# Attention logits from high and low float32r parts, outputs turned beside their accumulators, and logits alternating with transposes

## Chip, cores and metric

One core of a Trainium2 chip. The metric is the device time of one launch in microseconds (us); a comparison is made on the median of several runs.

## What is computed

A decoder layer on x of 2048 x 256: x = LN(x + attention(x)); x = LN(x + cross_attention(x, ctx)); x = LN(x + ffn(x)). The change concerns the first attention, of 16 heads of 64, whose logits carry a contextual position term (CoPE). For each head:

```python
sim = einsum('bid,bjd->bij', q, k) * d ** (-0.5)
G = sigmoid(sim); P = minimum(flip(cumsum(flip(G))), T_MAX - 1)
E = einsum('bnc,ct->bnt', q, pos_emb)
w = P - floor(P)
sim = sim + w * E[ceil(P)] + (1 - w) * E[floor(P)]
out = softmax(sim) @ v        # heads side by side, then @ Wout + b_out
```

All inputs are float32. Only the last 176 keys of a row have a position below the cap, so the kernel adds the term in a window of 176 columns (W).

## The kernel before

`attention()` works in 128 groups (G): 16 heads times 8 groups, each group being two units of 128 queries (u = 0, 1) against all 2048 keys. The five engines run hand-written programs side by side, tied by semaphores; nothing but these programs sets the order of the work. In PSUM, `Sc` has four banks of logits, `near` one bank of window logits, `ring` two banks used in turn by everything that ScalarE copies out, and `out` one accumulator bank.

For group g, in the order of TensorE's `body` (L581):

- `logits` (L544) of unit 0: one float32 matmul of 128 queries by 512 keys per bank. The head has 64 channels, so a matmul uses 64 rows of the array; even blocks of keys lie on partitions 0 to 63 and odd ones on 64 to 127 of `qk`, the queries `q_now` on both, and two matmuls on different row halves stand in a row. The wait for `exp_done` guards `Sc`, which the exponentials of the last unit still read.
- `turn` (L575) of unit 0 of group g-1: a matmul with `fold` adds and turns the two halves of its outputs into a `ring` bank. Then four times `transposes` (L552) of unit 1 of g-1, each of which fills a `ring` bank and waits until ScalarE has emptied the one before the last; `outputs` (L566), 16 matmuls into `out`, with `project` (L500) and `project_values` (L513) for a group 8 ahead after the first four.
- `logits` of unit 1, `turn` of unit 1 of g-1, four `transposes` of unit 0, `window` (L522) for group g+2, `outputs` of unit 0.

A group thus has two halves, one from unit 1's logits to unit 0's, one back.

ScalarE (`body` in its block) copies `out` to `halves` (L424), scales a turned output into `attn` (`scale`, L418), copies transposes to `probsT` (L409), copies a projection to `qk` (L368) and values to `V` (L382), takes a tanh of the window (L388), copies the table of position terms (L392), and does the exponentials (`exps`, L430) in two halves of 1024 columns when VectorE's `bias` (L765) is ready. VectorE takes maxima of 1024 columns (`half_max`, L748), adds the position term to the last columns (`add_window`, L755), and between these works through the position chain of the next group: scans (L674, L689), masks (L702), masked shifts (L712, L735) and small operations. GpSimd does one product per group (L348). SP issues the DMAs: `load_far` (L237) for the window's queries two groups ahead, `load_tile` (L258), and `load_now` (L241, L242), two DMAs that fill `q_now` for group g+1 once all logits of g are done:

```python
wait_apart(sp, bank_full, g * 4 + 4, waited)
load_now(g + 1, not odd)
```

Groups 112 to 119 project queries and keys alone, groups 120 to 127 nothing. Eight projection steps run ahead of the first group. TensorE's program for heads 1 to 12 is a loop over two heads, with `head` written out twice; each has an inner loop over two written-out bodies and two more bodies behind it, so that eight bodies are written out in it. After `attention()` come `general_attention()`, whose branches are not taken here, and `cross_and_ffn()`, from about 2180 us to the end; neither is touched.

## Time and profile before

| | us |
|---|---|
| median of 3 runs | 2649.62 (2647.76 to 2652.51) |
| the profiled execution's own time | 2652.94 |
| its span, first to last instruction | 2651.1 |
| TensorE busy (matmuls) | 2472.1, 93% |
| VectorE busy | 2006.4, 76% |
| ScalarE busy | 1615.9, 61% |
| GpSimd busy | 190.4, 7% |
| DMA engines, mean share | 10.1% |
| mean granted TensorE clock | 0.985 of 2.4 GHz |

Busy times are of the whole span; the first attention takes about 2177 us of it. A float32 matmul shows as two records and two weight loads, a transpose as one. Records of matmuls that follow one another overlap, so the time of a piece is read from its start to the start of the next.

### The profile page before, as it was taken

The page shows a single profiled execution, that of the slowest core. Times are in us where ns is not written, and L with a number is a line of the kernel's source. Part 1 is how long each engine was busy: PE and PEld are TensorE (multiplying, and loading weights), DVE is VectorE, ACT ScalarE, POOL GpSimd, SP SyncE. Part 2 cuts the span into 40 slices and gives each one's busy share as a digit, 9 for nine tenths or more (in the row PEclk, how much of TensorE's full clock was granted, in tenths as well). Part 3 has the DMA queues.
Part 4 walks back from the last instruction along what each step waited for, and adds up shares of the span by engine and source line. Part 5 has one row for each costly group of instructions (what it writes and reads, how often), then busy time and mean ns, then how long its engine had stood idle before and what let it go on. Part 6 is the DMA issues. An engine that isn't in the chain of part 4 may idle for free. (4 is left out here: it accounts for less than half of the span.)

```text
span 2651.1 us, 64197 instructions
## 1 busy us (share of the span) xinstructions
PE 2472.1 (93%) x18687; PEld 1691.1 (64%) x18687; DVE 2006.4 (76%) x5179; ACT 1615.9 (61%) x3383; POOL 190.4 (7%) x289
## 2 busy tenths in 40 slices
PE   7999998999899989998999999999999988999997
PEld 5666665666566656666666566666666656777776
DVE  6888888888888888888888888888899960232322
ACT  4666666666666666666666666666666663444442
POOL 0000000000000000000000000000000000111111
PEclk9999999999999999999999999999999998999998
DMA  2010101010101010100101110101001002100100
GB/s 68 20 33 20 34 20 32 20 34 20 32 20 34 20 32 21 32 21 21 29 24 29 25 29 24 29 24 29 22 21 40 21 17 68 34 26 34 36 26 6
DMA packets 96567, 74.74 MB, mean 28 GB/s; under 512 B 24590, under 2 KB 92303, under 8 KB 96464
## 3 DMA queue, kind: packets, MB, share of 16 engines
q1 hardware_dynamic: 96464, 73.15, 10.1%
q8 instruction: 90, 1.47, 0.2%
q14 instruction: 13, 0.11, 0.0%
HBM read 14.26 MB, written 2.10 MB: 6 GB/s over the span
## 5 line engine op out<-in xcount | busy, mean ns | idle before, releaser
L748 DVE TENSOR_REDUCE mx<-Sc 128x1 f32<-128x1024 f32 x512 | 621.5, 1214 | 160.2 <-PE Sc L544 159.7
L552 PE MATMUL ring<-ident,probs 128*128 128x128 f32 x4096 | 620.9, 284 | 115.2 <-ACT attn L418 65.3
L409 ACT ACTIVATE probsT<-ring 128x512 f32<-128x512 f32 x1024 | 584.7, 596 | 132.1 <-PE ring L552 129.2
L552 PEld LDWEIGHTS ring<-ident,probs 128*128 128x128 f32 x4096 | 446.3, 145 | 258.3 <-ACT attn L418 127.0
L430 ACT ACTIVATE probs<-Sc,nbias 128x1024 f32<-128x1024 f32 x512 | 565.6, 1117 | 4.7 <-DVE nbias L765 4.7
L544 PE MATMUL Sc<-qk,q_now 64*128 64x512 f32 x2048 | 539.4, 637 | 22.4 <-issue 16.0
L566 PE MATMUL out<-probsT,V_now 128*64 128x128 f32 x8192 | 530.0, 277 | 0.0
L566 PEld LDWEIGHTS out<-probsT,V_now 128*64 128x64 f32 x8192 | 439.5, 137 | 76.3 <-ACT probsT L409 57.9
L712 DVE COPY_PREDICATED z<-mask,z 128x224 f32<-128x224 int16 (+5 forms) x768 | 389.7, 507 | 34.4
L418 ACT ACTIVATE attn<-ring,rsum 128x64 f32 (+1 forms) x256 | 80.3, 314 | 436.5 <-PE ring L575 420.7
L544 PEld LDWEIGHTS Sc<-qk,q_now 64*128 64x128 f32 x2048 | 173.6, 188 | 217.8 <-issue 217.8
L348 POOL TENSOR_TENSOR prod<-cut,z 128x350 f32<-128x350 f32 x128 | 118.3, 924 | 2036.2 <-DVE z L735 2036.2
L575 PEld LDWEIGHTS ring<-fold,halves 128*128 128x128 f32 x512 | 76.9, 189 | 197.0 <-issue 114.6
L702 DVE TENSOR_SCALAR mask<-dist 128x352 int16<-128x352 int16 x896 | 155.3, 245 | 6.6
L500 PE MATMUL ring<-xT,wqk 128*128 (+1 forms) x512 | 144.3, 404 | 2.1 <-DMA wv<-in_L_attn_Wkv_dram 1.3
L522 PE MATMUL near<-qk,q_far 64*128 64x240 f32 x512 | 137.5, 389 | 2.0 <-DMA q_far<-qk 2.0
L674 DVE TENSOR_TENSOR_SCAN twoP<-tanh,ones 128x176 f32<-128x176 f32 x256 | 119.6, 510 | 12.6 <-ACT tanh L388 12.6
L735 DVE COPY_PREDICATED z<-mask,z 128x348 f32<-128x348 int16 x256 | 125.4, 544 | 0.1
L689 DVE TENSOR_TENSOR_SCAN rnd<-twos,rnd 128x176 f32<-128x176 f32 x256 | 118.9, 506 | 0.1
L424 ACT ACTIVATE halves<-out 128x128 f32<-128x128 f32 x256 | 72.1, 282 | 70.3 <-PE out L566 70.3
L575 PE MATMUL ring<-fold,halves 128*128 128x64 f32 x512 | 112.3, 301 | 1.6 <-ACT probs L430 1.2
L430 ACT ACTIVATION_READ_ACCUMULATOR probs<-Sc,nbias 128x1 f32 x512 | 108.1, 211 | 0.0
(116 smaller groups left out, 2301.8 us busy)
## 6 DMA issues: line engine op xcount, KB each, us to landing
q_now<-qk SPq DMA_DIRECT2D x256, 64.0 KB, 2.0
xv<-xT SPq DMA_DIRECT2D x113, 128.0 KB, 2.2
q_far<-qk SPq DMA_DIRECT2D x128, 64.0 KB, 1.9
V_now<-V SPq DMA_DIRECT2D x16, 512.0 KB, 3.2
at<-attn SPq DMA_DIRECT2D x16, 512.0 KB, 3.2
probs<-in_x_dram SPq DMA_DIRECT2D x4, 512.0 KB, 5.3
wqk<-in_L_attn_Wq_dram SPq DMA_DIRECT2D x32, 64.0 KB, 2.1
xin<-in_x_dram SPq DMA_DIRECT2D x16, 128.0 KB, 2.8
```

What stands on the lines that cost most here:

```text
L409: nc.scalar.activation(probsT[:, u, 4 * s:4 * s + 4, :], ring[k % 2][:, :].rearrange("p (t q) -> p t q", q=P), ACT.Copy).then_inc(slot_out, 1)
L430: nc.scalar.activation(probs[:, u, cols], Sc[:, cols], ACT.Exp, bias=nbias[:, u:u + 1], accum_out=sums[:, u, half:half + 1]).then_inc(exp_ ...
L500: last = nc.tensor.matmul(ring[k % 2][:, 0:STEP], wqk[:, c, at:at + 2 * C], xT[:, c, bass.ds(b * STEP, STEP)], start=c == 0, stop=c == DC - 1)
L522: last = nc.tensor.matmul(near[:, i * (W + T):(i + 1) * (W + T)], q_far[C:P, i * P:(i + 1) * P], qk[C:P, par, 1, HALF - W:QK], start=True, ...
L544: last = nc.tensor.matmul(Sc[:, bank * BANK:(bank + 1) * BANK], q_now[rows, u * P:(u + 1) * P], qk[rows, par, r, cols], start=True, stop=True)
L552: last = nc.tensor.transpose(ring[k % 2][:, j * P:(j + 1) * P], probs[:, u, (4 * s + j) * P:(4 * s + j + 1) * P], ident[:, :])
L566: last = nc.tensor.matmul(out[half:half + C, 0:P], V_now[:, token_tile(t), :], probsT[:, u, t, :], start=t < 2, stop=t >= NT - 2)
L575: nc.tensor.matmul(ring[k % 2][:, 0:C], halves[:, u, :], fold[:, :], start=True, stop=True).then_inc(slot_full, 1)
L702: nc.vector.tensor_scalar(mask[:, b, :, :], dist[:, :, :], 2 << b, None, ALU.bitwise_and).then_inc(shifted, 1)
L712: nc.vector.copy_predicated(z[:, 0, :, 0:k], mask[:, b, :, 0:k], z[:, 0, :, 1 << b:W]).then_inc(shifted, 1)
L735: last = nc.vector.copy_predicated(z[:, :, i, 1:W - 1], mask[:, 0, i, 1:W - 1].unsqueeze(1).broadcast_to([P, 2, W - 2]), z[:, :, i, 2:W])
L748: nc.vector.tensor_reduce(mx[:, u, half:half + 1], Sc[:, half * HALF:(half + 1) * HALF], AX.X, ALU.max).then_inc(dve_unit, 1)
```

## The change

- The queries and keys of a projection step go from `ring` to two tiles: `full`, plain float32, and `hi`, float32r (a rounded float32 format). GpSimd computes `lo` = `full` - `hi`. SP moves the four parts by DMA: queries to `q2`, high parts on partitions 0 to 63 and low ones on 64 to 127, keys in the same way to `kk`, whose last columns hold the table in the same two parts. `full`, `hi` and `lo` exist once.
- A logits bank is now two float32r matmuls on 128 rows: the high query parts (on both partition halves) with the keys' high and low parts, then the low query parts, added in PSUM. The same holds for the window, with 240 columns. `q_now` and `q_far` take four DMAs each. All keys of a head lie in order, so the odd and even groups are no longer different, and the loops on all engines run over single groups.
- GpSimd's subtraction waits until VectorE has done "shift 5", which stands before the first maximum of unit 1.
- `turn` writes columns 128 to 191 of `out`, not a `ring` bank, and moves behind the third transposes; `outputs` waits until ScalarE has scaled what was turned there. `scale` moves behind ScalarE's third copy.
- `logits` and `transposes` alternate by bank from the second bank on; the transposes of unit 0 wait for `hi_done` of the projection in the same ring bank.
- TensorE's `head` has an inner loop over one body and two more bodies: six written out in the loop over two heads.

```diff
-        qk = sb("qk", [P, 2, 2, QK])
-        qk_scale = sb("qk_scale", [P, 2])
+        kk = sb("kk", [P, 2, NTAB], F32R)
+        q2 = sb("q2", [P, 2, N], F32R)
+        full = sb("full", [P, STEP])
+        hi = sb("hi", [P, STEP], F32R)
+        lo = sb("lo", [P, STEP], F32R)
...
+                at = bass.ds(t * STEP, STEP)
+                for part in range(2):
+                    src = q2[part * C:(part + 1) * C, h % 2, at].bitcast(F32)
+                    for half in range(2):
+                        sp.dma_start(dst[half * C:(half + 1) * C, part, :].bitcast(F32), src).then_inc(landed, 16)
+
+            def load_far(g):
+                load_queries(q_far, g, far_in)
+
+            def load_now(g):
+                load_queries(q_now, g, now_in)
+
+            def move(s):
+
+                h, b = s // PAIRS, (s + 7) % PAIRS
+                at = bass.ds(b * STEP, STEP)
+                for part, src in enumerate((hi, lo)):
+                    rows = slice(part * C, (part + 1) * C)
+                    sp.dma_start(q2[rows, h % 2, at].bitcast(F32), src[0:C, :].bitcast(F32)).then_inc(moved, 16)
+                    sp.dma_start(kk[rows, h % 2, at].bitcast(F32), src[C:P, :].bitcast(F32)).then_inc(moved, 16)
...
+            for s in range(PAIRS):
+                sp.wait_ge(lo_done, s + 1)
+                move(s)
+                if s == 1:
+                    sp.wait_ge(moved, 2 * 64)
+                    load_far(0)
+                    load_now(0)
+                if s == 4:
+                    sp.wait_ge(moved, 5 * 64)
+                    sp.wait_ge(near_full, 1)
+                    load_far(1)
...
-            def body(g, odd, late=False, first=False, tile=True, far=True, head=False):
+            def body(g, late=False, first=False, tile=True, far=True, head=False):
                 base = slots_before(g, late)
+                if far:
+
+                    wait_apart(sp, near_full, g + 2, waited)
+                    wait_apart(sp, moved, (G if late else g + 4) * 64, waited)
+                    load_far(g + 2)
                 if head:
 
                     wait_apart(sp, out_full, g * 2, waited)
                     load_values(g)
-                if far:
-
-                    wait_apart(sp, near_full, g + 2, waited)
-                    wait_apart(sp, slot_out, 8 + 2 * PAIRS if first else base - 4, waited)
-                    load_far(g + 2, odd)
                 if tile:
-                    wait_apart(sp, slot_full, base + Slots(first).values + 1, waited)
+                    wait_apart(sp, slot_full, base + Slots().values + 1, waited)
                     load_tile(g + 1)
+                if not late:
+                    wait_apart(sp, lo_done, g + (PAIRS + 1), waited)
+                    move(g + PAIRS)
                 wait_apart(sp, bank_full, g * 4 + 4, waited)
-                load_now(g + 1, not odd)
-
-            body(0, False, first=True)
-            body(1, True)
-            with sp.Fori(2, PAIRS, 2) as g:
-                body(g, False)
-                body(g + 1, True)
+                load_now(g + 1)
...
+            def remainder(s, beside=None):
+
+                pool.wait_ge(hi_done, s + 1)
+                if beside is not None:
+                    pool.wait_ge(moved, s * 64)
+                    wait_apart(pool, shifted, beside * CH + (CHAIN.index("shift 5") + 1), waited)
+                elif s:
+                    pool.wait_ge(moved, s * 64)
+                nc.gpsimd.tensor_tensor(lo[:, :], full[:, :], hi[:, :].bitcast(F32),
+                                        ALU.subtract).then_inc(lo_done, 1)
+
+            def slope_product(c):
                 pool.wait_ge(shifted, c * CH + CH)
                 nc.gpsimd.tensor_tensor(prod[:, :, 1:W], frac[:, :, 1:W], z[:, 1, :, 1:W],
                                         ALU.mult).then_inc(prod_done, 1)
 
-            with pool.Fori(0, G) as c:
-                body(c)
+            for s in range(PAIRS):
+                remainder(s)
+            slope_product(0)
+            with pool.Fori(0, LASTP) as g:
+                remainder(g + PAIRS, g + 1)
+                slope_product(g + 1)
...
-            def project(s, odd, base, k, alone=False):
-
-                h, b = s // PAIRS, (s + 7) % PAIRS
+            def project(s, base, k, alone=False):
+
                 act.wait_ge(slot_full, base + k + 1)
-                nc.scalar.activation(qk[:, h % 2, int(odd), bass.ds(b // 2 * STEP, STEP)], ring[k % 2][:, 0:STEP],
-                                     ACT.Copy, scale=qk_scale[:, int(odd):int(odd) + 1])\
+                if not (isinstance(s, int) and s == 0):
+                    act.wait_ge(lo_done, s)
+                    wait_apart(act, moved, s * 64, waited)
+                nc.scalar.activation(full[:, :], ring[k % 2][:, 0:STEP], ACT.Copy, scale=qk_scale[:, :])\
                     .then_inc(slot_out, 2 if alone else 1)
+                nc.scalar.activation(hi[:, :], ring[k % 2][:, 0:STEP], ACT.Copy, scale=qk_scale[:, :]).then_inc(hi_done, 1)
...
-            def scale(g, u, base, k):
+            def scale(g, u):
 
                 h, t = g // PAIRS, g % PAIRS
                 act.wait_ge(rsum_done, g * 2 + u + 1)
-                wait_apart(act, slot_full, base + k + 1, waited)
-                nc.scalar.activation(attn[:, t * 2 + u, bass.ds(h * C, C)], ring[k % 2][:, 0:C], ACT.Copy,
-                                     scale=rsum[:, u:u + 1]).then_inc(slot_out, 1)
+                wait_apart(act, turned, g * 2 + u + 1, waited)
+                nc.scalar.activation(attn[:, t * 2 + u, bass.ds(h * C, C)], out[:, TURN:TURN + C], ACT.Copy,
+                                     scale=rsum[:, u:u + 1]).then_inc(scaled, 1)
...
-                    scale(g - 1, 0, base, at.turn0)
-                    transposed(1, base, at.last)
+                    transposed(1, base, at.last, range(3))
+                    scale(g - 1, 0)
+                    transposed(1, base, at.last, range(3, 4))
...
+                transposed(0, base, at.now, range(3))
                 if not first:
-                    scale(g - 1, 1, base, at.turn1)
-                transposed(0, base, at.now)
+                    scale(g - 1, 1)
+                transposed(0, base, at.now, range(3, 4))
...
-                    last = nc.tensor.matmul(near[:, i * (W + T):(i + 1) * (W + T)], q_far[C:P, i * P:(i + 1) * P],
-                                            qk[C:P, par, 1, HALF - W:QK], start=True, stop=True)
+                    for part in range(2):
+                        last = nc.tensor.matmul(near[:, i * (W + T):(i + 1) * (W + T)],
+                                                q_far[:, part, i * P:(i + 1) * P], kk[:, par, TAIL:NTAB],
+                                                start=part == 0, stop=part == 1)
                 last.then_inc(near_full, 1)
...
-            def logits(par, u, half):
-
-                cols = slice(half * BANK, (half + 1) * BANK)
-                for r in range(2):
-                    rows = slice(r * C, (r + 1) * C)
-                    bank = half * 2 + r
-                    last = nc.tensor.matmul(Sc[:, bank * BANK:(bank + 1) * BANK], q_now[rows, u * P:(u + 1) * P],
-                                            qk[rows, par, r, cols], start=True, stop=True)
-                last.then_inc(bank_full, 1)
+            def logits(par, u, bank):
+
+                cols = slice(bank * BANK, (bank + 1) * BANK)
+                for part in range(2):
+                    last = nc.tensor.matmul(Sc[:, cols], q_now[:, part, u * P:(u + 1) * P], kk[:, par, cols],
+                                            start=part == 0, stop=part == 1)
+                if bank % 2:
+                    last.then_inc(bank_full, 1)
...
+                    if turned_before:
+                        wait_apart(pe, scaled, g * 2 + u, waited)
...
-            def turn(g, u, base, k):
+            def turn(g, u):
 
                 pe.wait_ge(halves_out, g * 2 + u + 1)
-                pe.wait_ge(slot_out, base + k - 1)
-                nc.tensor.matmul(ring[k % 2][:, 0:C], halves[:, u, :], fold[:, :],
-                                 start=True, stop=True).then_inc(slot_full, 1)
-
-            def body(g, odd, par, late=False, first=False, proj=True, val=True, far=True, far_par=None):
+                nc.tensor.matmul(out[:, TURN:TURN + C], halves[:, u, :], fold[:, :],
+                                 start=True, stop=True).then_inc(turned, 1)
...
-                pe.wait_ge(now_in, g * 32 + 32)
-                if first:
-                    pe.wait_ge(slot_out, 8 + 2 * PAIRS)
+                at = Slots(proj)
+                pe.wait_ge(now_in, g * 64 + 64)
+                wait_apart(pe, moved, (g // PAIRS * PAIRS + PAIRS) * 64, waited)
                 if not first:
                     wait_apart(pe, exp_done, g * 4 - 1, waited)
                 logits(par, 0, 0)
-                if not first:
-                    wait_apart(pe, exp_done, g * 4, waited)
                 logits(par, 0, 1)
                 if not first:
-                    turn(g - 1, 0, base, at.turn0)
-                    for s in range(4):
-                        transposes(1, base, at.last, s)
+                    transposes(1, base, at.last, 0)
+                    wait_apart(pe, exp_done, g * 4, waited)
+                logits(par, 0, 2)
+                if not first:
+                    transposes(1, base, at.last, 1)
+                logits(par, 0, 3)
+                if not first:
+                    transposes(1, base, at.last, 2)
+                    turn(g - 1, 0)
+                    transposes(1, base, at.last, 3)
                     outputs(g - 1, 1, base, at.last, tiles=range(FIRST))
                 if proj:
-                    weights_at = (g // PAIRS) * 64 + 128 if val else H * 64 - 16
-                    project(g + PAIRS, not odd, base, at.qk, weights_at, alone=not val)
+                    weights_at = (g // PAIRS) * 48 + 96 if val else H * 48 - 16
+                    project(g + PAIRS, base, at.qk, weights_at, alone=not val)
                 if val:
                     project_values(g + PAIRS, base, at.values)
                 if not first:
                     outputs(g - 1, 1, base, at.last, tiles=range(FIRST, NT))
                 wait_apart(pe, exp_done, g * 4 + 1, waited)
                 logits(par, 1, 0)
+                logits(par, 1, 1)
+                if proj:
+                    wait_apart(pe, hi_done, g + (PAIRS + 1), waited)
+                transposes(0, base, at.now, 0)
                 wait_apart(pe, exp_done, g * 4 + 2, waited)
-                logits(par, 1, 1)
+                logits(par, 1, 2)
+                transposes(0, base, at.now, 1)
+                logits(par, 1, 3)
+                transposes(0, base, at.now, 2)
                 if not first:
-                    turn(g - 1, 1, base, at.turn1)
-                for s in range(4):
-                    transposes(0, base, at.now, s)
+                    turn(g - 1, 1)
+                transposes(0, base, at.now, 3)
                 if far:
                     pe.wait_ge(near_out, g * 2 + 4)
                     window(g + 2, par if far_par is None else far_par)
-                outputs(g, 0, base, at.now, empty=not first)
+                outputs(g, 0, base, at.now, empty=not first, turned_before=not first)
...
             def head(at, par, start=0, **kw):
 
-                with pe.Fori(start, PAIRS - 2, 2) as t:
-                    body(at + t, False, par, **kw)
-                    body(at + t + 1, True, par, **kw)
+                with pe.Fori(start, PAIRS - 2) as t:
+                    body(at + t, par, **kw)
```

TensorE's queue, the half of a group that begins with unit 1's logits, before (L66 is the helper that waits; x2 are two matmuls):

```order
L66 REGISTER_ALU
L544 MATMUL Sc<-qk,q_now 128x512 x2
L66 REGISTER_ALU
L544 MATMUL Sc<-qk,q_now 128x512 x2
L573 REGISTER_ALU
L574 REGISTER_ALU
L575 MATMUL ring<-fold,halves 128x64
L550 REGISTER_ALU
L552 MATMUL ring<-ident,probs 128x128 x4
```

The same place in the changed kernel (L67 is the same helper):

```order
L568 MATMUL Sc<-kk,q_now 128x512 x4
L67 REGISTER_ALU
L575 REGISTER_ALU
L577 MATMUL ring<-ident,probs 128x128 x4
L67 REGISTER_ALU
L568 MATMUL Sc<-kk,q_now 128x512 x2
L575 REGISTER_ALU
L577 MATMUL ring<-ident,probs 128x128 x4
L568 MATMUL Sc<-kk,q_now 128x512 x2
```

The last two banks of logits now stand behind the first transposes, and these behind the wait for `hi_done` (the first L67 after the four matmuls).

SP's queue, one group, before (an L241 or L242 row is one half of `q_now`):

```order
L237 DMA q_far<-qk 64x256
L66 REGISTER_ALU
L258 ISA
L258 DMA xv<-xT 128x2x128
L66 ISA
L241 ISA x2
L241 DMA q_now<-qk 64x256
L242 DMA q_now<-qk 64x256
```

In the changed kernel, from behind the load of `xv` on:

```order
L251 ISA
L251 DMA q<-hi 64x256
L252 ISA
L252 DMA kk<-hi 64x256
L251 ISA
L251 DMA q<-lo 64x256
L252 ISA
L252 DMA kk<-lo 64x256
L67 ISA
L237 ISA
L237 REGISTER_ALU
L237 DMA q_now<-q 64x256 x2
```

Four moves, each of half a tile, have come between the load of `xv` and the loads of `q_now`, of which there are four (two more behind this piece) where there were two.

## Rows read from the trace of the kernel before

**Rows 1.** Windows: stretch, length, busy PE, PEld, DVE, ACT, POOL, clock, DMA share, GB/s

```profile
60.00:1961.00 1901.00, 1777.97 (x14434) 1189.84 (x14434) 1666.10 (x4291) 1259.77 (x2706) 104.45 (x113) 0.99 0.10 26
...
2059.00:2166.00 107.00, 101.44 (x847) 64.67 (x845) 99.24 (x252) 73.10 (x154) 6.47 (x7) 1.00 0.06 15
```

**Rows 2.** Timeline, GpSimd: start, us, instruction, idle time before it

```profile
1031.38 0.92 POOL L348 TENSOR_TENSOR prod<-cut,z 128x350 f32<-128x350 f32 x1 [15.67 <-DVE z L735]
...
2019.03 0.93 POOL L348 TENSOR_TENSOR prod<-cut,z 128x350 f32<-128x350 f32 x1 [15.11 <-DVE z L735]
...
2112.55 0.92 POOL L348 TENSOR_TENSOR prod<-cut,z 128x350 f32<-128x350 f32 x1 [14.43 <-DVE z L735]
```

**Rows 3.** Timeline, TensorE and its weight loads, one group of the long stage

```profile
1005.70 1.99 PE L544 MATMUL Sc<-qk,q_now 64*128 64x512 f32 x8
1007.61 0.43 PE L575 MATMUL ring<-fold,halves 128*128 128x64 f32 x2
...
1008.69 1.15 PE L552 MATMUL ring<-ident,probs 128*128 128x128 f32 x8 [0.20 <-ACT attn L418]
...
1010.62 1.07 PE L522 MATMUL near<-qk,q_far 64*128 64x240 f32 x4
1011.62 1.97 PE L566 MATMUL out<-probsT,V_now 128*64 128x128 f32 x32
...
1013.52 0.30 PEld L544 LDWEIGHTS Sc<-qk,q_now 64*128 64x128 f32 x4 [0.17 <-issue]
...
1013.52 2.14 PE L544 MATMUL Sc<-qk,q_now 64*128 64x512 f32 x8
1015.59 0.43 PE L575 MATMUL ring<-fold,halves 128*128 128x64 f32 x2
...
1016.82 1.15 PE L552 MATMUL ring<-ident,probs 128*128 128x128 f32 x8 [0.35 <-ACT attn L418]
...
1018.74 0.66 PE L566 MATMUL out<-probsT,V_now 128*64 128x128 f32 x8
...
1022.30 1.99 PE L544 MATMUL Sc<-qk,q_now 64*128 64x512 f32 x8
```

**Rows 4.** Timeline, VectorE, the same group

```profile
1008.42 0.34 DVE L755 TENSOR_TENSOR Sc<-Sc,prod 128x175 f32<-128x175 f32 x1
...
1018.79 0.15 DVE L765 TENSOR_REDUCE nbias<-mx 128x1 f32<-128x2 f32 x1
...
1023.47 1.23 DVE L748 TENSOR_REDUCE mx<-Sc 128x1 f32<-128x1024 f32 x1 [1.13 <-PE Sc L544]
```

**Rows 5.** Waits of TensorE up to 2200 us; GpSimd's row behind one of them

```profile
PE Sc L544 <- issue: 16.0, 5, 3.5
...
998.10 0.93 POOL L348 TENSOR_TENSOR prod<-cut,z 128x350 f32<-128x350 f32 x1 [22.07 <-DVE z L735]
```

**Rows 6.** Timeline, TensorE, cross attention: float32 matmuls on 128 rows

```profile
2402.78 1.88 PE L1504 MATMUL Sc<-K2T,QT 128*128 128x512 f32 x4
```

**Rows 7.** Timeline, all engines, the start

```profile
14.57 0.47 ACT L368 ACTIVATE qk<-ring,qk_scale 128x256 f32<-128x256 f32 x1 [1.33 <-PE ring L500]
...
30.69 1.99 PE L544 MATMUL Sc<-qk,q_now 64*128 64x512 f32 x8 [0.56 <-ACT V L375]
...
38.89 0.15 DVE L765 TENSOR_REDUCE nbias<-mx 128x1 f32<-128x2 f32 x1
...
39.08 1.11 ACT L430 ACTIVATE probs<-Sc,nbias 128x1024 f32<-128x1024 f32 x1 [4.67 <-DVE nbias L765]
```

**Rows 8.** Timeline, ScalarE: exponentials of a late group; copies of the long stage

```profile
2101.77 1.12 ACT L430 ACTIVATE probs<-Sc,nbias 128x1024 f32<-128x1024 f32 x1
...
2103.95 0.29 ACT L424 ACTIVATE halves<-out 128x128 f32<-128x128 f32 x1
...
1022.91 0.47 ACT L368 ACTIVATE qk<-ring,qk_scale 128x256 f32 x1 [0.22 <-issue]
1023.36 0.28 ACT L382 ACTIVATE V<-ring 128x128 f32 x1
```

**Rows 9.** SP's queue in the long stage, and the page's DMA issues (median us to landing)

```profile
1024.74 0.48 SPq L241 DMA_DIRECT2D q_now<-qk  x1
1025.27 0.60 SPq L242 DMA_DIRECT2D q_now<-qk  x1
...
q_now<-qk SPq DMA_DIRECT2D x256, 64.0 KB, 2.0
```

More of the change, by code:

```diff
@@ L330, in _ @@
+            body(G - 2, late=True, tile=False, far=False)
         @block.gpsimd
@@ L402, in _, with transposed @@
                     near_tanh(1)
-            def transposed(u, base, slots):
-                for s in range(4):
+            def transposed(u, base, slots, part=range(4)):
+                for s in part:
                     k = slots[s]
@@ L633, in _ @@
             head(LASTP, 1, late=True, proj=False, val=False)
-            body(G - 2, False, 1, late=True, proj=False, val=False, far=False)
-            body(G - 1, True, 1, late=True, proj=False, val=False, far=False)
+            body(G - 2, 1, late=True, proj=False, val=False, far=False)
+            body(G - 1, 1, late=True, proj=False, val=False, far=False)
             base, at = slots_before(G, True), Slots(proj=False)
             pe.wait_ge(exp_done, 4 * G)
-            turn(G - 1, 0, base, at.turn0)
-            for s in range(4):
-                transposes(1, base, at.last, s)
+            for n in range(4):
+                transposes(1, base, at.last, n)
+                if n == 2:
+                    turn(G - 1, 0)
             outputs(G - 1, 1, base, at.last)
-            turn(G - 1, 1, base, 5)
+            turn(G - 1, 1)
         @block.vector
```

197 lines of the change are left out of this document (87 added, 110 removed).

## Prediction

> **What bounds the kernel now.** I read the stretches first, then TensorE's timeline over one group, then the same group on VectorE, ScalarE and GpSimd, then the DMA queue. Between 60 and 1961 us TensorE is busy 1778 of 1901 us at granted clock 0.99, i.e. its 2.4 GHz level, VectorE 1666 [rows 1]. The reader should see there that both are near full, so taking work off TensorE can gain only what VectorE leaves. GpSimd runs one product per group, so its idle time plus its length is the period: 15.67 + 0.92 = 16.6 us in the long stage, 16.04 in the eight groups with a query/key projection but no values, 15.35 in the last eight, without either [rows 2]. In those last groups VectorE is busy 99.2 of 107 us with only instruction gaps left [rows 1]: about 15.3 us is the period below which this VectorE work doesn't go. The long stage has 110 periods.
>
> In the long stage TensorE never rests but for four gaps per group: 0.20 and 0.19 us in the first half, 0.35 and 0.20 in the second, 0.94 together, all before transposes that wait for ScalarE to empty a ring bank [rows 3], where one of each half stands. The first half (logits of unit 1 to logits of unit 0) takes 7.82 us, the second 8.78. VectorE waits once, 1.13 us, for unit 1's logits [rows 4].
>
> One thing lies outside the period: five times TensorE's logits wait for "issue", 16.0 us in all, and GpSimd then shows a period of 22.07 + 0.93 = 23.0 instead of 16.6 [rows 5]. The five (22.8, 21.4, 23.0, 21.5, 22.5) come every 16 groups, where TensorE's outer loop over two heads jumps back, and cost 28 us together. Its inner jumps, over two written-out bodies, cost nothing.
>
> **The change, part by part.**
>
> *Logits.* Before, a bank is one float32 matmul on 64 rows, and two run side by side: four banks, 1.91 us in the first half and 2.07 in the second [rows 3]. Now a bank is two float32r matmuls on all 128 rows, one after the other. No row has a float32r price. The upper bound is plain float32 on 128 rows: four records of 128x512 (two matmuls) take 1.88 us [rows 6], 0.94 each, 7.5 us per unit. The lower is one column per clock, 512 / 2.4 = 0.213 us, 1.7 us per unit. I take the lower: the kernel now splits its operands into high and low parts itself, for which there is no use if the engine still worked at full precision. To that I add 0.11 us where a group of matmuls begins, an estimate between 0 and the 0.19 of one weight load (0.30 for the four of a pair, overlapping): the first load of a group starts with its matmul and not ahead of it [rows 3]. A bank costs 0.54, the first two together 0.97. So the logits alone gain nothing; the pairing given up costs what the cheaper type brings.
> [...]
>
> *Window.* Two matmuls on 64 rows (1.00 us from its start to the outputs' [rows 3]) become four on 128 rows, 240 columns: four times 0.10 and 0.2 for the start, 0.60. Upper bound, at the float32 price: 4 x 0.94 x 240/512 = 1.76.
>
> *Alternation.* The transposes come one slot (0.57 us, half of 1.15 for eight [rows 3]) per 0.54 us of logits, so ScalarE's copies (0.60) keep up and the 0.94 us of gaps go. The turned output leaves the ring; outputs now wait for its scaling, which hides under the last slot but for 0 to 0.3 us.
>
> *Sum on TensorE.* Second half: 0.97 + 4 x 0.58 + 2 x 0.54 + turn 0.27 + the unchanged 3.56 from outputs to the next logits [rows 3] = 8.20. First half: 0.97 + 2.32 + 1.08 + 0.27 + window 0.60 + outputs 1.90 = 7.14. Together 15.3. That is also VectorE's floor, so without new waits 1.3 us of each group would go. There are new waits.
>
> *The copies full and hi.* ScalarE now empties the projection twice, and TensorE's first transposes of unit 0 wait for hi_done. Unit 1's last two banks are queued behind those transposes, and VectorE waits for them. The ring closes like this, from VectorE's bias of unit 0: 0.19 to the exponential [rows 7]; 2.18 for both halves and to the copy of the halves [rows 8]; that copy 0.28; full 0.45 (ScalarE's distance from the old copy to the next instruction), hi 0.47, perhaps the 0.22 "issue" gap before it [rows 8]; 0.1; transposes, logits, transposes, logits 2.24; 0.17 until VectorE starts (1.13 idle against 0.95 of matmuls); and from add-window to the next bias 10.37 [rows 4]. Sum 16.45, or 16.67 with the gap.
>
> *Low parts and moves.* From the end of hi: 0.1, GpSimd's subtraction 924 ns x 256/350 = 0.68 [rows 2] (up to 0.92), 0.15; then SP's queue: four moves and four loads of q_now, where before there was one far load far ahead and two q_now loads, 0.53 us apart [rows 9]. Seven distances of 0.55 are 3.85, landing 2.0 after the last issue [rows 9], 0.1: unit 0's next logits can start 6.9 us after hi. Then 8.20 of TensorE, 0.1, and halves, gap, full, hi 1.42: 16.6. In the kernel before, the second q_now load was issued at 1025.27 and landed at 1027.3, some 3 us before its use at 1022.30 + 7.82, so SP did not matter; now it is a ring as long as the other. xv and q_far stand behind these on SP, and have half a period of slack. GpSimd's subtraction falls 3.7 to 4.5 us after bias, inside the maximum of unit 1's first half (in the late groups it begins 3.5 us after it and takes 1.22): it costs VectorE nothing; without that cover it would stand beside a masked copy, where the 1 us that VectorE then waits takes it up.
>
> TensorE's own ring, with 0.66 us waiting for hi, is 16.0. Two rings at 16.5 to 16.6: I take **16.6**, so 110 periods give back what they gained: 0. The eight groups without values go from 16.04 to about 16.55, +4. The last eight stay at VectorE's 15.3: 0.
>
> *Start.* The eight first steps took about 2 us each, from ScalarE's first copy at 14.57 to the logits at 30.69 [rows 7]. Now full, hi and lo are single buffers, and each step's copy waits until the last step's moves have landed: 0.45 + 0.47 + 0.1 + 0.7 + 0.1 + 3 x 0.53 + 2.0 + 0.1 = 5.5. Seven steps, the first to its landing (5) and eight loads of q_far and q_now between (3) put the logits at 14.6 + 5 + 38.5 + 3 = 61. VectorE, which had its first bias 8.2 us after the first logits since it was still preparing, is ready by then and needs 4.5: first bias at 65.7 against 38.89 [rows 7], **+27 us**.
>
> *Outer loop.* TensorE's loop over two heads falls from eight written-out bodies to six. Bounds for its 28 us: all gone or all kept. Two bodies jump free, eight don't; six lie nearer to eight, but what costs is code that does not stay, and with a quarter less of it all may stay; then only a part of one jump is left. I take **-25**.
>
> *Sum:* +27 + 4 - 25 + 0 = +6. The profiled execution took 2652.94 us, 3.3 above the median of 2649.62; on the median, **2656**.
>
> **Rivals.**
> 1. *The rings close sooner, and the kernel is faster.* Place: the chain bias, exponentials, halves, full, hi, second logits. If the 0.22 gap isn't there and a bank costs 0.45, the first ring is 16.27. For it: the waits before full are long met. Against: the SP ring must be as short too, with issues of 0.50. At 16.3: -33 - 2, gives 2621. It decides from a period of 16.55 down. Chance 0.25.
> 2. *The jump stays.* Then 2656 + 25 = 2681. For it: six bodies are nearer to eight than to two. Chance 0.22.
> 3. *The window's 240 columns cost the float32 price,* 1.16 us more: TensorE's ring is 17.2, 118 x 0.6 = +70, 2726. The same result comes if a bank costs 0.8. Chance 0.12.
> 4. *Float32r makes two passes:* +3.4 us on TensorE's ring, 19.4, +2.8 x 118, about 2990. Chance 0.06.
> 5. *The new waits are hidden, and VectorE's 15.35 is reached* (what the order of the code aims at): -1.25 x 110 with the start and the loop as above, some 2515. Against: both rings. Chance 0.03.
>
> **How the numbers follow.** My forecast, 2656 (2640 to 2668 by itself), has 0.32. About 0.2 per cent, 5.3 us, can be told from no change. Faster: 0.22 of rival 1, 0.03 of rival 5, 0.03 of mine, 0.28. Same: 0.10 of mine, 0.03 of rival 1, 0.13. Slower: 0.59. The range runs from 2618, just below rival 1, to 2715, into rival 3; outside lie rivals 4 and 5 and parts of 1 and 3, about 0.19.
>
> **What would show it.** GpSimd's product every 16.6 us; its subtraction, about 0.7 us, inside VectorE's first maximum of unit 1. TensorE idle about 0.66 us before the transposes of unit 0, released by hi, and no longer for ring banks. VectorE waiting before add-window of unit 1 for the logits, about 1 us, rather than before the maximum. First logits near 61 us. No period over 20 us at the outer jump. A float32r record of 512 columns lasting more than 0.3 us from start to start would make it wrong, as would q_now arriving over 7.2 us after hi, or a period below 16.3.

## The result and the profile after

The changed kernel takes **3023.87 us** (median of 4, 3018.41 to 3025.38) where the kernel before takes 2651.07 on the same chip: a ratio of 1.1407 (95% interval 1.1385 to 1.143), 373 us more. Of the kernel before's four runs one took 3486.99 us and the others 2647.76 to 2652.51. The forecast was 2656 us, in a range from 2618 to 2715. Slower was the likelier side; the size was missed by far.

The page of the changed kernel (span 3023.6 us, mean granted clock 0.933 where it was 0.985): busy time of the engines, loads of instructions, and the costliest group:

```profile
PE 2437.8 (81%) x18687; PEld 1981.4 (66%) x18687; DVE 2011.0 (67%) x5181; ACT 1670.1 (55%) x3511; POOL 285.0 (9%) x415
...
q8 instruction: 36, 0.59, 0.1%
...
L568 PE MATMUL Sc<-kk,q_now 128*128 128x512 f32 x2048 | 764.0, 479 | 388.1 <-DMA q_now<-q 373.8
```

The last row points at the loss: TensorE stood 373.8 us idle before its logits, until q_now landed. That a wait is as large as the loss is no proof that it is the loss, and here it is not quite: the product of GpSimd, which comes once in a group, lets the time be laid out by stages.

| stage | before | after | difference | forecast |
|---|---|---|---|---|
| to the second product | 50.95 | 85.94 | +35.0 | +27 |
| long stage, 111 periods | 1871.6 | 2190.5 | +318.9 | -25 (outer loop) |
| 8 groups without values | 128.7 | 145.3 | +16.6 | +4 |
| last 7 periods | 106.1 | 108.5 | +2.4 | 0 |

Of the 111 periods 85 last 19.2 to 20.7 us, 24 last 17.6 to 18.6 and two are longer; before, 106 lasted 16.3 to 16.7 and five longer. Both kinds stand side by side in one trace. The windows of two groups (stretch, length, busy time of PE, PEld, DVE, ACT, POOL, clock, DMA share, GB/s), each cut at the first logits of a unit:

```profile
1006.30:1016.50 10.20, 6.70 (x64) 5.49 (x62) 8.22 (x19) 6.58 (x15) 0.83 (x2) 1.00 0.29 70
1016.50:1026.40 9.90, 9.15 (x66) 7.62 (x66) 6.81 (x20) 5.01 (x10) 0.83 (x1) 0.83 0.20 48
1026.44:1036.42 9.98, 6.69 (x64) 5.52 (x63) 7.89 (x19) 6.59 (x15) 0.73 (x1) 1.00 0.41 119
1036.42:1044.67 8.25, 7.57 (x67) 6.31 (x67) 6.64 (x21) 5.01 (x10) 0.94 (x1) 1.00 0.14 31
```

The half that begins behind the wait does the same work in both groups. At the 2.4 GHz level (clock 1.00) it takes 8.25 us, the forecast's 8.20; where the clock has fallen to its 1.2 GHz level for part of it (mean 0.83) it takes 9.90. The timeline shows that level at the same place (start, us, instruction, idle time before it in brackets):

```profile
1016.57 1.18 PE L568 MATMUL Sc<-kk,q_now 128*128 128x512 f32 x4 [3.10 <-DMA q_now<-q]
...
1018.01 1.20 PE L568 MATMUL Sc<-kk,q_now 128*128 128x512 f32 x2
...
1019.72 1.20 PE L568 MATMUL Sc<-kk,q_now 128*128 128x512 f32 x2
...
1036.42 1.16 PE L568 MATMUL Sc<-kk,q_now 128*128 128x512 f32 x4 [2.81 <-DMA q_now<-q]
...
1037.78 0.71 PE L568 MATMUL Sc<-kk,q_now 128*128 128x512 f32 x2
...
1038.68 0.70 PE L568 MATMUL Sc<-kk,q_now 128*128 128x512 f32 x2
```

Two logits matmuls are a record of 0.70 us in the one and 1.20 in the other. In this group the level does not fall during the wait, but 1.3 us after TensorE has started again: the first record of four lasts 1.18 us and 1.16, nearly the same, and the next windows read 1.00 and then 0.51:

```profile
1016.50:1017.80 1.30, 1.23 (x6) 1.03 (x7) 0.02 (x1) 0.00 (x0) 0.83 (x1) 1.00 0.41 99
1017.80:1021.30 3.50, 3.50 (x15) 2.90 (x14) 1.98 (x4) 1.20 (x2) 0.00 (x0) 0.51 0.41 98
```

TensorE had been idle for 2.81 us before the one half and 3.10 before the other, but the length of the wait does not tell the two kinds apart. In groups 1 to 112, 24 kept the 2.4 GHz level; 15 of them had waited 3.08 to 3.15 us, as most of the others had. Of the 88 that lost it, 13 had waited only 2.31 to 2.90 us.

Now the wait itself. The chain from hi to q_now, in ScalarE's, GpSimd's and SP's rows of the first group:

```profile
1007.11 0.47 ACT L394 ACTIVATE hi<-ring,qk_scale 128x256 fp32r<-128x256 f32 x1
...
1007.93 0.73 POOL L359 TENSOR_TENSOR lo<-full,hi 128x256 fp32r<-128x256 f32 x1 [10.58 <-ACT hi L394]
...
1009.12 0.51 SPq L251 DMA_DIRECT2D q<-hi  x1
...
1009.83 0.50 SPq L252 DMA_DIRECT2D kk<-hi  x1
...
1010.47 0.49 SPq L251 DMA_DIRECT2D q<-lo  x1
...
1011.11 0.49 SPq L252 DMA_DIRECT2D kk<-lo  x1
...
1012.18 2.41 SPq L237 DMA_DIRECT2D q_now<-q  x4
```

From the end of hi (1007.58) to the logits (1016.57) pass 9.0 us; in the group with the full clock 8.70 (1027.72 to 1036.42). The forecast had 6.9. Piece by piece: to the first move 1.54 (forecast 0.93), the four moves and the step to the first load 3.06 (2.20), three more loads some 1.9 (1.65), from there to the logits some 2.5 (2.1). So every piece of SP's queue was longer, none of them by more than 0.9 us.

The start: ScalarE's second, third and last copy of the eight steps and TensorE's first logits, against 14.57 and 30.69 [rows 7]:

```profile
22.22 0.47 ACT L392 ACTIVATE full<-ring,qk_scale 128x256 f32<-128x256 f32 x1 [4.56 <-DMA kk<-lo]
...
27.89 0.47 ACT L392 ACTIVATE full<-ring,qk_scale 128x256 f32<-128x256 f32 x1 [4.55 <-DMA kk<-lo]
...
60.85 0.47 ACT L392 ACTIVATE full<-ring,qk_scale 128x256 f32<-128x256 f32 x1 [4.19 <-DMA kk<-lo]
...
66.58 3.75 PE L568 MATMUL Sc<-kk,q_now 128*128 128x512 f32 x8 [6.70 <-DMA kk<-lo]
```

### The profile page after: what moved, and what is told of

Same layout as the page of the kernel before. It is cut to its first block and busy times, and to the rows that moved or that the text cites. A ratio compares the mean times of both kernels' runs of the same rounds, so it can differ in the third digit from the quotient of the medians.

```text
span 3023.6 us, 67656 instructions
## 1 busy us (share of the span) xinstructions
PE 2437.8 (81%) x18687; PEld 1981.4 (66%) x18687; DVE 2011.0 (67%) x5181; ACT 1670.1 (55%) x3511; POOL 285.0 (9%) x415
## 5 line engine op out<-in xcount | busy, mean ns | idle before, releaser
L568 PE MATMUL Sc<-kk,q_now 128*128 128x512 f32 x2048 | 764.0, 479 | 388.1 <-DMA q_now<-q 373.8
L433 ACT ACTIVATE probsT<-ring 128x512 f32<-128x512 f32 x1024 | 610.7, 597 | 815.2 <-PE ring L577 815.2
L577 PE MATMUL ring<-ident,probs 128*128 128x128 f32 x4096 | 697.1, 298 | 43.3 <-ACT V L406 38.2
L577 PEld LDWEIGHTS ring<-ident,probs 128*128 128x128 f32 x4096 | 559.8, 159 | 213.6 <-ACT V L406 84.3
L568 PEld LDWEIGHTS Sc<-kk,q_now 128*128 128x128 f32 x2048 | 375.0, 216 | 463.3 <-issue 437.4
L796 DVE TENSOR_TENSOR Sc<-Sc,prod 128x175 f32<-128x175 f32 x256 | 89.2, 348 | 220.3 <-PE Sc L568 216.6
L359 POOL TENSOR_TENSOR lo<-full,hi 128x256 fp32r<-128x256 f32 x128 | 93.4, 730 | 1283.2 <-ACT hi L394 1283.2
L524 PEld LDWEIGHTS ring<-xT,wqk 128*128 128x128 f32 x512 | 89.4, 194 | 49.3 <-issue 41.9
L454 ACT ACTIVATION_READ_ACCUMULATOR probs<-Sc,nbias 128x1 f32 x512 | 100.2, 196 | 0.0
L1542 PE MATMUL Sc<-K2T,QT 128*128 128x512 f32 (+1 forms) x256 | 98.5, 519 | 1.2 <-ACT QT L1461 1.2
```

Source lines behind the costliest of these rows:

```text
L433: nc.scalar.activation(probsT[:, u, 4 * s:4 * s + 4, :], ring[k % 2][:, :].rearrange("p (t q) -> p t q", q=P), ACT.Copy).then_inc(slot_out, 1)
L454: nc.scalar.activation(probs[:, u, cols], Sc[:, cols], ACT.Exp, bias=nbias[:, u:u + 1], accum_out=sums[:, u, half:half + 1]).then_inc(exp_ ...
L524: last = nc.tensor.matmul(ring[k % 2][:, 0:STEP], wqk[:, c, :], xT[:, c, bass.ds(b * STEP, STEP)], start=c == 0, stop=c == DC - 1)
L568: last = nc.tensor.matmul(Sc[:, cols], q_now[:, part, u * P:(u + 1) * P], kk[:, par, cols], start=part == 0, stop=part == 1)
L577: last = nc.tensor.transpose(ring[k % 2][:, j * P:(j + 1) * P], probs[:, u, (4 * s + j) * P:(4 * s + j + 1) * P], ident[:, :])
L1542: last = nc.tensor.matmul(Sc[:, lo:lo + w], QT[:, c, :], K2T[:, c, lo:lo + w], start=c == 0, stop=c == DC - 1)
```

## The experiments

Code is shown in short, with the statements that change alone. Theory Q: the period is the ring hi, low parts, SP's eight transfers, logits, hi. Theory K: on top of it the clock falls because of the wait. The rival to both is ring 1, from bias through ScalarE's copies back to VectorE's maxima, or TensorE's new order of work. All medians stand against 2648 to 2650 us for the kernel before on the same chip.

### 1. SP loads q_now before the moves

```
-    wait lo_done; move(g + PAIRS); wait bank_full; load_now(g + 1)
+    wait bank_full; load_now(g + 1); wait lo_done; move(g + PAIRS)
```

> Theory Q (SP's queue: q_now is issued last of eight DMAs behind the low parts, and TensorE idles 3.1 us per group for it): q_now is now issued as soon as all logits are done, about 1.3 us earlier and with nothing ahead of it, and is there before the outputs end. TensorE's wait for q_now falls from 374 us to under 40; what is left is a wait of about 3 us for the moves at each head's first group. Period near 17, time 2700 to 2780. Theory K (the idle also drops TensorE's clock): granted clock back from 0.93 to 0.98 or more. Theory R (the float32r logits and their alternation with transposes are the costly part): TensorE's work is the same, time stays above 2950.

Measured 2735.92 us (2732.51 to 2738.28), ratio 1.0326 (1.0301 to 1.0352), clock 0.972 (0.98 was expected): 288 us come back by swapping two statements. Most periods are 16.4 to 16.8 us. Its waits between 80 and 2150 us (total us, times, longest):

```profile
PE Sc L568 <- ACT probs L454: 95.0, 76, 1.6
...
PE Sc L568 <- DMA kk<-lo: 61.1, 15, 4.4
...
PE Sc L568 <- DMA q_now<-q: 32.8, 28, 2.1
```

The moves are now late instead, but only the first group of a head needs them at once (15 times, 61 us). Theory Q holds.

### 2. Two q_now buffers, loaded a group ahead

```
-    q_now = sb("q_now", [P, 2, 2 * P], F32R)
+    q_now = sb("q_now", [P, 2, 2, 2 * P], F32R)     # bodies in pairs, 8 written out
```

> Two buffers for q_now, filled a whole group ahead; TensorE's bodies are written out in pairs, eight in the loop over two heads as before the change. Q: no wait for q_now and none at the heads' first groups; what remains is the ring through full, hi and the last two logits banks, period 16.6 to 16.9, plus 36 us at the start and the 28 us of the outer jump back again if eight bodies are too many: 2690 to 2740. R: above 2950.

Measured 2627.15 us (2624.32 to 2628.91), ratio 0.9914 (0.989 to 0.9938): with the wait away the change is 0.9% faster than the kernel before, more than I had expected. 103 of the 111 periods read 16.0 to 16.2 us. What is left is ring 1, with a period 0.3 to 0.5 us under the forecast's 16.45 to 16.67:

```profile
DVE Sc L807 <- PE Sc L577: 105.0, 125, 1.8
PE ring L586 <- ACT V L415: 94.0, 106, 1.1
...
PE Sc L577 <- DMA q_now<-q: 18.4, 5, 3.9
```

TensorE's transposes of unit 0 wait for ScalarE's copies of the projections (0.89 us each time, until the copy of V behind full and hi; forecast 0.66, for hi), two banks of logits stand behind them, and VectorE waits 0.84 us for those. With eight written-out bodies, the page counts 90 loads of instructions as before (36 after the change), and five periods of over 20 us are back.

### 3. Thin and dense matmuls in the wait

```
+    for n in range(12): matmul(near[:, 480:512], ident, fold[:, 0:32])      # thin
+    for n in range(12): matmul(ring[0][:, 0:P], ident, ident)               # dense
```

> The changed kernel with 12 small matmuls (128x32, into unused columns of near) ahead of each wait for q_now; the wait itself still ends when q_now lands. K (the clock falls because TensorE idles 3 us): granted clock in the second half back from 0.83 to near 1, that half from 9.9 to about 8.8 us, period 19.0, time 2890 to 2940. If the slow second half has another cause: 3020 or above.

> The changed kernel with 12 float32 matmuls of 128x128 into an idle ring bank in TensorE's wait ahead of the logits (some 2.9 us, dense, where the earlier filler of 32 columns was thin). Theory K (the second half is 9.9 instead of 8.2 us long because the clock falls while TensorE waits): granted clock of that half 0.95 or more, its length 8.4 to 8.9, period 18.7 to 19.2: 2870 to 2930 us. Rival N (the half is long by its own waits, or the clock falls whatever stands there): period stays at 20 or grows by what the filler overruns: 3010 to 3080 us.

Thin: 3059.84 us (3053.61 to 3063.49), ratio 1.1541 (1.1512 to 1.1571), clock 0.930. The records cover the gap (24 in 2.87 us), yet the logits behind them run at the low level:

```profile
1024.63 2.87 PE L653 MATMUL near<-fold,ident 128*128 128x32 f32 x24
1027.83 1.39 PE L568 MATMUL Sc<-kk,q_now 128*128 128x512 f32 x4 [0.33 <-issue]
...
1029.72 1.20 PE L568 MATMUL Sc<-kk,q_now 128*128 128x512 f32 x2
```

That run alone would have spoken against theory K. Dense: 2919.21 us (2917.42 to 2921.83), ratio 1.1021 (1.0999 to 1.1043), clock 0.981:

```profile
1020.09 2.94 PE L652 MATMUL ring<-ident 128*128 128x128 f32 x24
1023.27 1.18 PE L568 MATMUL Sc<-kk,q_now 128*128 128x512 f32 x4 [0.24 <-issue]
...
1024.64 0.72 PE L568 MATMUL Sc<-kk,q_now 128*128 128x512 f32 x2
```

The same 24 records in the same 2.9 us, but of 128 columns, hold the clock, and the half behind them takes 8.32 us (1023.27 to 1031.59). Of the 112 halves behind the wait 4 are at the low level here, 92 with the thin filler and 88 with none. The first thing that follows: **useless work on TensorE saves 105 us** here. The second: the logits still start 9.0 us after hi (1014.25 to 1023.27), and the long stage is still 220 us longer than before the change (2091.9 against 1871.6). Both fillers also make TensorE's body longer. The page then counts 80 loads of instructions where the changed kernel has 36, and five waits of 2.2 to 3.0 us for "issue" stand where the outer loop jumps back, some 13 us in all: part of the 36 us that the thin filler loses. TensorE is busy for 90% of this run's span and the kernel is 10% slower than before; a high busy share proves nothing.

### 4. GpSimd issues the moves of the low parts

```
-    SP:   wait lo_done; 4 moves
+    SP:   wait hi_done; 2 moves of hi       GpSimd: lo; wait lo_done; 2 moves of lo
```

> The changed kernel, but the two moves of the low parts are issued by GpSimd, right behind its subtraction, and SyncE starts the two moves of the high parts when hi is there. Theory Q (the changed kernel's period is the chain from hi through SyncE's own instructions to q_now): of the 9.0 us from the end of hi to the logits, the subtraction (0.35 + 0.73) and two of the moves (2 x 0.65) leave the chain, 2.4 us. Period 20.1 -> 17.7, and down to 16.6 to 17 if the clock no longer falls, since TensorE is then idle for less than 1 us: 2650 to 2770 us. Rival D (not SyncE's issuing but the transfers' own time, or crowded DMA engines, make q_now late): the same eight transfers run, the period stays above 19.5: 2960 us or more.

Measured 2696.21 us (2687.33 to 2721.82), ratio 1.0191 (1.0121 to 1.0261), clock 0.982: 328 us less than the changed kernel, with the same eight transfers. One group, SP's and GpSimd's queues and TensorE:

```profile
1001.07 0.73 POOL L363 TENSOR_TENSOR lo<-full,hi 128x256 fp32r<-128x256 f32 x1 [7.74 <-ACT hi L404]
1001.09 0.51 SPq L250 DMA_DIRECT2D q<-hi  x1
...
1002.65 0.56 POOL L368 DMA_DIRECT2D q<-lo  x1 [0.85 <-POOL lo L363]
...
1003.40 2.42 SPq L238 DMA_DIRECT2D q_now<-q  x4
...
1007.93 1.17 PE L578 MATMUL Sc<-kk,q_now 128*128 128x512 f32 x4 [1.40 <-ACT probs L464]
```

Its runs lie further apart than others, so against the kernel before it is 1 to 3% slower; against the changed kernel the gain is clear. The logits come 7.3 us after hi (1000.63), and what they wait for last is ScalarE's exponential, not q_now. Crowded transfers are not the cause: the same eight run, and a load of q_now lands 2.0 us after its issue on the profile's pages of the kernel before, of the changed one and of this one. What has gone from SP's queue ahead of q_now is two issues and the wait for GpSimd's subtraction; this run doesn't part the two. The Trainium skill (DMA: Bandwidth & Descriptors, Issuing engines are not separate DMA queues) says that issuing from several engines saves only the sequencer's time to initiate, "usually small relative to the DMA itself". The saving here is of that kind, with the wait for the subtraction beside it, and not small where eight issues lie in a ring: 10.8% of the changed kernel's time, the clock that it brings back included.

### 5. The alternation of logits and transposes, undone twice

```
-    logits 0, 1, T0, logits 2, T1, logits 3, T2, turn, T3
+    logits 0, 1, 2, 3, T0, T1, T2, turn, T3
```

> The changed kernel without the alternation: all four logits banks, then the four transposes. Q: the DMA chain starts at the copies of the projection and is as long as now, so within 1 per cent of 3024 (2990 to 3050). R: if alternating is what costs, it falls by more than 50 us.

> The version with two q_now buffers (2627 us), with its four banks of logits in a row and its transposes behind them, as the kernel before orders them. Theory A (the alternation lets ScalarE's copies and VectorE's maxima run beside TensorE; it was worth 95 us in the changed kernel): 2680 to 2740 us. Rival V (without the wait for q_now, VectorE's own queue of 16.0 us a group is the bound and hides the order of TensorE): 2615 to 2650 us.

In the changed kernel: 3118.7 us (3115.77 to 3121.62, 2 runs), ratio 1.1771 (1.1735 to 1.1808), 95 us slower, clock 0.921, outside what was expected. Its periods are 20.2 to 20.7 us nearly throughout. The traces place 90 us, all in the long stage. Behind the wait, 108 of 112 halves lose the high level where 88 did, which is some 32 us (20 x 1.6), and each of these halves is about 0.4 us longer, some 45. The other halves add 13, most of it in the groups where the outer loop jumps back: five periods there last 22.7 to 23.1 us, and the page counts 72 loads of instructions against 36, with the same six bodies. In the version of experiment 2: 2575.33 us (2573.1 to 2576.02), ratio 0.9726 (0.9707 to 0.9744), 52 us **faster**, against both theories. There the four banks cover ScalarE's copies, the wait for V and VectorE's wait before add-window are gone from its list, and the period is 15.6 to 15.8:

```profile
1014.87 2.15 PE L577 MATMUL Sc<-kk,q_now 128*128 128x512 f32 x8
...
1016.04 0.28 ACT L415 ACTIVATE V<-ring 128x128 f32 x1
...
1016.86 1.03 PE L586 MATMUL ring<-ident,probs 128*128 128x128 f32 x8
```

### 6. VectorE's clamp and fractions on GpSimd

```
-    VectorE: clamp (0.34 us), fractions (0.51 us)
+    GpSimd:  clamp, subtract RND2, subtract
```

> The version with two q_now buffers, with the clamp (0.34 us) and the fractions (0.51 us) of the positions taken from VectorE and given to GpSimd as three operations, two beside a maximum of VectorE. Theory V (VectorE is busy for 15 to 15.5 us of each 16.15: its queue is the bound there): period 15.4 to 15.8, 2540 to 2600 us. Rival R (ring 1, from bias through ScalarE and TensorE back to the maxima, is the bound, and VectorE just fills it): period stays at 16.1, 2615 to 2635 us. Rival S (GpSimd and VectorE slow each other down): VectorE's operations are longer, 2640 us or more.

Measured 2621.16 us (2620.15 to 2624.76), ratio 0.9901 (0.9881 to 0.9922): 6 us for 0.85 us a group taken off VectorE. Ring 1 binds (R). The maxima kept their 1209 ns, so S did not show; but the clamp, which took VectorE 337 ns, takes GpSimd 1395, and a single subtraction of the same size 1097:

```profile
L378 POOL TENSOR_SCALAR cut<-twoP 128x352 f32<-128x352 f32 x124 | 173.0, 1395 | 283.2 <-DVE rnd L770 283.2
L380 POOL TENSOR_SCALAR whole<-rnd 128x352 f32<-128x352 f32 x124 | 136.0, 1097 | 9.8
```

### 7. Towards the best version: the start, the outer loop

All on the unalternated version with two buffers (2575.33 us).

```
+    start: full, hi, lo [P, 2, STEP], a semaphore for each buffer's moves      # s_cn_start
-    for h in 1, 3, 5 ...: head(h, 1); head(h + 1, 0)
+    for h in 1, 2, 3 ...: head(h, parity from a register)                      # o_one_head
```

> The version with two q_now buffers and unalternated logits (2575 us); in the eight steps of the start, full, hi and lo have two buffers each, so that ScalarE need not wait until the moves of the step before have landed. Theory P (the start grew because each step is the chain full, hi, lo, four moves, landing, 5.65 us): a step falls to the issuing of its moves, 4 x 0.65 = 2.6 us, with 12 loads of 0.65 between; first logits at 45 to 50 instead of 66: 2553 to 2563 us. Rival (the start is bound by loads of weights or by code): first logits stay above 60, 2570 to 2580 us.

> The same version (2575 us) with the parity of the key table held in a register, so that TensorE's outer loop has one head of four written-out bodies instead of two heads (eight bodies). Theory J (with eight bodies the jump back of the outer loop costs TensorE 4 to 5 us each time, six times): periods above 20 us are gone, 25 to 30 us less: 2545 to 2552 us. Rival M (an address from a register costs each of the 40 logits and window matmuls of a group some 20 ns): 128 x 40 x 0.02 = 100 us more: 2640 to 2680 us.

> Both of the two before together: 2525 to 2540 us if both hold and add up.

> Both of the two before, and the clamp and the fractions on GpSimd. In the alternated version that gave 6 us, although it took 0.85 us a group off VectorE. Theory R (ring 1 binds, VectorE only fills it): 5 us or less from it: 2520 to 2540 us. Rival V (without the alternation ring 1 is 0.5 us shorter, so that VectorE's queue is the bound there and gives 0.3 us or more a group): 2480 to 2505 us.

| version | us (lowest to highest) | ratio (interval) | first logits | instruction loads |
|---|---|---|---|---|
| two buffers, unalternated | 2575.33 (2573.1 to 2576.02) | 0.9726 (0.9707 to 0.9744) | 64.06 | 90 |
| with the start | 2559.47 (2554.13 to 2560.75) | 0.9661 (0.9641 to 0.9682) | 50.82 | 90 |
| with one head | 2554.92 (2552.12 to 2558.36) | 0.9646 (0.9628 to 0.9664) | 64.32 | 26 |
| **with both** | **2544.18** (2543.48 to 2544.44) | 0.9609 (0.9592 to 0.9626) | 51.80 | 26 |
| both, and 6 | 2548.4 (2542.99 to 2555.42) | 0.9629 (0.9602 to 0.9656) | 50.46 | 26 |

The start gives 16 us and the outer loop 20; registers in the addresses of the 20 logits and window matmuls of a group cost little: leaving out the jumps, the mean period is 15.80 us against 15.70, so that some 27 us at the jumps come back and some 12 are lost elsewhere. Rival M had taken 100. Together they give 31, a little less than the sum and less than I expected. Moving work off VectorE still gives nothing, so rival V falls here too; what binds this version at 15.7 us stays open. The version with both, 2544 us, beats the kernel before by 3.9% and the changed kernel by 16%.

## Why the prediction was wrong

**The step that failed** is the sum of *Low parts and moves*: "seven distances of 0.55 are 3.85 ... unit 0's next logits can start 6.9 us after hi". It measured 8.7 to 9.0 us. The ring itself was the right one and was in the forecast, only as "a ring as long as the other", so its 2 us of error went straight into each of some 118 periods. The experiments show it: a shorter way to q_now took 288 us off (1) and 328 (4), a second buffer 397 (2). The distance of 0.53 came from two loads in a row of the same helper, both without a wait [rows 9]. In the changed queue the moves are 0.64 to 0.71 us apart, 0.90 to 1.07 us lie from the last move to the first load, where SP passes a wait and works out new addresses, and 0.46 between the end of the subtraction and the first move. The text had set its own alarm, "q_now arriving over 7.2 us after hi", and the alarm was right.

**What had no step at all** is the clock. With 8.7 to 9.0 us from hi to q_now TensorE is idle for about 3 us once a group, and in 88 of the 112 groups its clock falls to the low level behind that: 9.84 us on average in place of 8.25. That is 140 us. The dense filler gives nearly all of it back (the halves behind the wait take 132 us less in sum), but puts 31 on the others. The other part: 9.0 or 8.7 + 8.25 + 1.28 (logits to the end of hi, 1006.30 to 1007.58) = 18.2 to 18.5 against 16.6, some 200 us over 111 periods. With the 28 of the outer loop off, 140 + 200 - 28 = 312 of the 319 measured. An error of 2 us in a wait cost 3.5 us in most groups, since with a wait of that size the clock fell.

Point by point:
- *Periods*: the long stage has 111, not 110.
- *Bank of logits* 0.54, the first two 0.97: measured 0.55 and 1.00 (logits at 1004.68, transposes at 1005.68, logits at 1006.03, transposes at 1006.58, in the dense filler's run). Eight float32r matmuls of 512 columns in a row start 0.25 us apart (1.97 us for eight, 1006.26 to 1008.23 in the unalternated version). Two records of plain float32 for the same 512 columns take 0.94 us [rows 6], nearly four times as long. The Trainium skill (FP8 and Floating Point Precision, TensorE Precision Notes) gives true FP32 four passes through the array; the ratio agrees with one pass for float32r. Rival 4 gave 2990 us, near the result, by a mechanism that did not occur (two passes).
- *Window* 0.60: 0.81 us from its start to the outputs' (1010.69 to 1011.50), a term 0.2 too low, with a record of 0.69 us for four matmuls. Rival 3 had 1.76; it falls.
- *TensorE's halves* 8.20 and 7.14: at full clock they take 8.25 and, without the wait, 7.17 (9.98 less 2.81). Errors cancel in them: a slot of transposes between banks is 0.36 us and not 0.58, and outputs wait 0.5 to 0.7 us for probsT, where 0 to 0.3 was taken.
- *Ring 1* 16.45 to 16.67: 16.0 to 16.2 in experiment 2, where nothing else binds. Rival 1 had named a shorter ring 1, but not for its reason: a bank costs 0.55, not 0.45; the two slots of transposes in the ring are 0.4 us shorter than taken. It was useless without the other ring.
- *Start* +27: +35. The first copy comes 1.9 us later (16.47), a step takes 5.67 us (5.5), and the loads between took longer than 3 us: one step with eight of them takes 8.95.
- *Groups without values* +4: +16.6, the same ring as in the long stage. *Last groups* 0: +2.4. The first of these periods is still long (18.95); the next five take 15.1 us each, which is under the 15.3 that the prediction called VectorE's floor.
- *Outer loop* -25: the outliers of the long stage fell from five to two, only one of them at a jump, and instruction loads from 90 to 36. With eight bodies both come back (experiment 2); with four the loads are 26 and the longest period 17.5 us, or 19.4 in the version with both. Rival 2 falls for this kernel. But six bodies are not safe: the fillers (80 loads) and the unalternated order (72) have six as well, and five long periods each.
- The alternation, costed as a gain of 0.94 us of gaps, loses 52 us once nothing else binds, because it puts a wait for ScalarE's copies between the banks that VectorE needs.

Still open: why 24 groups keep the clock and 88 lose it behind waits of the same length, why six bodies are loaded again in some orders, and how much of the 0.46 to 1.07 us at a wait on SP is the wait and how much the address arithmetic.

## What to carry to other kernels

Count a queue's issues as instructions: when a change puts transfers ahead of a load that somebody waits for, price each issue, wait and new address on that queue by its like, and if two rings come out equal, price the error of the one that you have measured least. Before anything is tuned, try the swap: loading what is needed next before storing what is needed a head later gave back 288 of 373 us without a byte of memory, and a second buffer gave more than the rest. Look at the granted clock by stretch as well as by mean: here a wait of some 3 us on TensorE cost about half as much again, 1.6 us, behind it in most groups.

## What was not expected of the hardware

- Behind waits of the same length, 3.08 to 3.15 us, the clock kept its 2.4 GHz level in 15 groups and fell in most others, and in the group shown it fell only after 1.3 us of new work. In the wait, 24 records of 32 columns did not keep it up (3059.84 us), 24 of 128 columns in the same 2.9 us did (2919.21 us).
- Moves issued by GpSimd cost it 0.52 to 0.56 us each and start 0.85 us after the subtraction; SP needs 0.46 for the same step.
- GpSimd took 1.40 us for the clamp on 128x352 that VectorE does in 0.34, and 1.10 for a subtraction of a constant.
